# A quarter of the gate additions as matrix products, and background work spread over the steps, in a fused two-attention kernel

## The chip, the cores and the metric

The kernel runs on all 8 cores of one Trainium2 chip. Each core computes one of the 8 sequences with all weights; the cores don't talk to each other. The time is that of the slowest core, in device microseconds (us).

## The reference

One sequence has 2048 tokens of 1024 features. In short:

```
x = x + attn_a(layernorm(x))
x = x + ffn(layernorm(x))        # W rounded to 4 bits, bias, a rank-16 term
x = x + attn_b(layernorm(x))     # causal, 16 heads, rotary
x = x + ffn(layernorm(x))

attn_a, for each of 8 heads, q and k in two halves of 64, each of length 1:
  L1 = (q1 . k1) * c ;  L2 = (q2 . k2) * c          # 2048 x 2048
  G  = tanh(gain * (L1 - L2))                       # the gate
  A1 = softmax(L1 + G) ;  A2 = softmax(L2 - G)
  y  = (A1 - lam * A2) @ v ; y = y / rms(y) * w ; out = y @ Wo.T + bo
```

The change lies in attn_a: its two gate additions are L1 + G and L2 - G.

## The kernel before, in words

Each core goes through these stages: LayerNorm and the projections Q, K, V; the first attention (attn_a); the projections of the second attention; the second attention. The output projection of attn_a, the first ffn and the LayerNorms around them run as background work inside the first attention, for one pair of blocks of 128 tokens at a time.

PE is TensorE, DVE is VectorE, ACT is ScalarE, POOL is GpSimd. The program writes out the order of each engine's instructions by hand (`Seq`); `wait` makes the engine's queue wait for a semaphore, `done` returns the token to wait for. An engine works in this order strictly.

The first attention has 64 units: a head and 256 queries (`QA`). A unit has 8 steps (`NKS`) of 256 keys each, so there are 512 steps, and the 8 units (64 steps) of one group of 256 queries complete one pair of token blocks. Step s does the following, at different iterations of one loop:

- `step_D`: two products on PE give `pD`, the difference L1 - L2 times the gain, 128 keys x 512 columns (2 groups of keys x 256 queries). There is one `pD`. The factor is in `Qn`, made by `make_qn` on POOL.
- `step_tanh`: ACT writes `Gt`, the gate, from `pD`.
- `step_L`: four products of 64 rows on PE give L1 in bank `pL[2 * (s % 2)]` and L2 in the bank behind it, 128x512 each. They wait until the additions of step s - 2 have read these banks.
- `step_S`: DVE writes `Sx`, L1 + G and L2 - G, with two operations of 128x512.
- `step_exp`: ACT writes `E` from `Sx`, 128x1024 in one instruction.
- `step_Y`: eight products on PE add E's product with the values V to `pY`. At k = 1 of each unit no such products are issued, at k = 2 those of two steps.

At the end of a unit `y_out` copies `pY` to `Yt` on DVE, POOL normalizes it, `y_rms` sums squares on DVE, and `turn` transposes the result into Q by a DMA of SyncE's queue (SP). After eight units `turn` puts a generator `after_a` into the background.

A `Background` object runs these generators. A generator yields a cost after each piece: 1 for a product of 128x512, 0.3 for a small one, 0 to say that the rest of the work is for a later step. `step(budget)` takes pieces until the budget is used or a 0 comes. `out_proj` has 9 products, then an addition to x and LayerNorm statistics on DVE, for each half of a block; `ffn` has 8 small products, then 9 wide ones for each half. `layer_norm` computes the scale on POOL and applies it some steps later, on ACT, and for the last pair on DVE. At first the background holds `quantize` and `prepare`, which round the ffn's weights to 4 bits and scale Wo on DVE.

The order of the loop's work before (from `for s in range(-3, NS + NKS)`) is: tanh(s+2), exp(s), Y(s-1), one background step of budget 3, D(s+3), L(s+2), S(s+1). The background of the last pair runs in the next stage with a budget of 9, and the second attention has a background of its own with 3.

Of the kernel before, what the change touches and what calls it, by code (L numbers as in the profile page):

```python
# [33 lines left out]
E_RING = 4  # L34
# [185 lines left out]
class Background:  # L220
# [3 lines left out]
    def __init__(self):  # L224
        self.gens = deque()
        self.calls = []
        self.clock = 0

    def add(self, gen):
        self.gens.append(gen)  # L230
# [1 line left out]
    def later(self, steps, fn):  # L232
        self.calls.append((self.clock + steps, fn))

    def step(self, budget):
        self.clock += 1
        due = [c for c in self.calls if c[0] <= self.clock]
        self.calls = [c for c in self.calls if c[0] > self.clock]
        for _, fn in due:
            fn()  # L240
        while self.gens and budget > 0:
            cost = next(self.gens[0], None)
            if cost is None:
                self.gens.popleft()
                return
            if cost <= 0:
                return
            budget -= cost

    def drain(self):  # L250
        while self.gens or self.calls:
            self.step(1e9)


def build_program():
# [23 lines left out]
    dram_in("fb", (16, D))  # L279
    dram_in("cosb", (128, T))  # L280
    dram_in("sinbs", (128, T))
    for w in ("tri", "perm", "blk"):
        dram_in(w, (128, 128))
    d_out = nc.dram_tensor("out", [T, D], F32, kind="ExternalOutput").ap()
    d_x2 = nc.dram_tensor("x2", [T, D], F32, kind="Internal").ap()
# [389 lines left out]
    zz = sb("zz", (128, 2, 128), F32, s2a)  # L675
    yt = [sb(f"yt{i}", (128, 2, 128), BF16, s2a) for i in range(3)]
    cu = [sb(f"cu{i}", (128, 12), F32, s2a) for i in range(2)]
    p2 = contextlib.ExitStack()
    pL = [ps(f"pL{i}", p2) for i in range(4)]
    pD = ps("pD", p2)  # L680
# [1 line left out]
    pB = ps("pB", p2)  # L682

    ac.add(lambda e: e.preload_act_table_set("exp_and_others"))
    pe.wait(c2_tok)
    for ap, val in ((lora[0][0:96, :], 1.0), (lora[0][96:128, :], 0.0), (lora[1][0:96, :], 1.0),
                    (lora[1][96:128, :], 0.0), (sel[0:96, :], 0.0), (sel[96:128, :], 1.0),
                    (fbb[:, :], 0.0)):
# [66 lines left out]
    def out_proj(b, y_toks, w_tok, bias):  # L755

        tok = slice(128 * b, 128 * (b + 1))
        pe.wait(w_tok, *y_toks)
        for hf in range(2):
            cols = slice(512 * hf, 512 * (hf + 1))  # L760
            bank = state["banks"].take(pe)
            for c in range(NCH):
                mm(pe, bank[0], Q[:, c, tok], Wo[:, c, cols], c == 0, c == NCH - 1 and not bias)
                yield 1
            if bias:
                pe.wait(state["row97"])
                mm(pe, bank[0], sel[:, :], fbb[:, cols], False, True)
            p_tok = pe.done()
            yield 0
            ve.wait(p_tok, x_tok[b])  # L770
            tt(ve, x[:, b % 4, cols], bank[0], x[:, b % 4, cols], OP.add)
            bank[1] = ve.done()
            ve.wait(bank[1])
            ln_stats(b, hf)
            yield 0

    def layer_norm(b, q, i, then):


        g_tok = ln_aggr(b)  # L780

        def scale():
            po.wait(g_tok)
            ts(po, st[:, b, 14:15], st[:, b, 13:14], LN_EPS, OP.add)
            po.wait(po.done())
            tt(po, st[:, b, 15:16], st[:, b, 14:15], mhalf, OP.pow)
            tt(po, st[:, b, 16:17], st[:, b, 12:13], mone, OP.mult)
            po.wait(po.done())
            tt(po, st[:, b, 17:18], st[:, b, 16:17], st[:, b, 15:16], OP.mult)
            s_tok = po.done()  # L790
            bg.later(2, lambda: apply(s_tok))

        def apply(s_tok):
            q.wait(s_tok, xm_free[i])
            if q is ac:
                act(ac, xm[i], x[:, b % 4, :], AF.Identity, scale=st[:, b, 15:16],
                    bias=st[:, b, 17:18])
            else:
                ts(ve, xm[i], x[:, b % 4, :], st[:, b, 12:13], OP.subtract,
                   st[:, b, 15:16], OP.mult)  # L800
            then(q.done())

        bg.later(1, scale)
# [7 lines left out]
    def ffn(b, slot):  # L811

        nonlocal n_lora
        xt = xnT[:, :, 128 * slot:128 * (slot + 1)]
        while b not in xT_tok:
            yield 0
        pe.wait(xT_tok[b], state["wq"], state["row97"])
        k = n_lora % 2
        n_lora += 1
        bank = state["banks"].take(pe)  # L820
        for c in range(NCH):
            mm(pe, bank[0][0:16, 0:128], fab[:, c, :], xt[:, c, :], c == 0, c == NCH - 1)
            yield 0.3
        p_tok = pe.done()
        yield 0
        ve.wait(p_tok, lora_free[k])
        copy(ve, lora[k][0:16, :], bank[0][0:16, 0:128])
        bank[1] = l_tok = ve.done()
        yield 0
        for hf in range(2):  # L830
            cols = slice(512 * hf, 512 * (hf + 1))
            bank = state["banks"].take(pe)
            for c in range(NCH):
                mm(pe, bank[0], xt[:, c, :], wq[:, c, cols], c == 0, False)
                yield 1
            pe.wait(l_tok)
            mm(pe, bank[0], lora[k][:, :], fbb[:, cols], False, True)
            p_tok = pe.done()
            yield 0
            ve.wait(p_tok)  # L840
            stt(ve, x[:, b % 4, cols], bank[0], qscale[:, 0:1], x[:, b % 4, cols],
                OP.mult, OP.add)
            bank[1] = ve.done()
            ve.wait(bank[1])
            if state["ln3"]:
                ln_stats(b, hf)
            yield 0
        lora_free[k] = xT_free[slot] = p_tok
        state["x"] = bank[1]

    x2_tok = [None] * NTB
    xn3_tok = [None] * NTB
# [8 lines left out]
    def after_a(n, y_toks):  # L861

        last = n == NTB // 2 - 1
        q = ve if last else ac
        two = (2 * n, 2 * n + 1)
        if not last:
            load_x(di["xN"], 2 * n + 2)
            load_x(di["xN"], 2 * n + 3)
        for i, b in enumerate(two):
            yield from out_proj(b, y_toks, state["Wo"], True)  # L870
            layer_norm(b, q, i, lambda a_tok, b=b, i=i: turn_ln(b, i, a_tok, b % 4))
        if last:
            state["last_o"](pe.done())
        for i, b in enumerate(two):
            yield from ffn(b, b % 4)
            sy.wait(state["x"])
            x2_tok[b] = r_st.next(sy).start(sy, rows_of(d_x2, b), x[:, b % 4, :])
            layer_norm(b, q, 2 + i, lambda a_tok, b=b, i=i: keep(b, 2 + i, a_tok))
        while xn3_tok[two[1]] is None:
            yield 0  # L880
# [2 lines left out]
    bg = Background()  # L883
    units = [(t, qs, h) for t in range(NQT) for qs in range(2) for h in range(HA)]
    NS = len(units) * NKS
    L_tok, D_tok, G_tok, S_tok, E_tok = {}, {}, {}, {}, {}
    Y_tok, y_evac, yn_tok, qn_tok, yt_tok, zz_tok = {}, {}, {}, {}, {}, {}

    def q_range(u):
# [3 lines left out]
    def make_qn(u):  # L893
# [4 lines left out]
        tt(po, Qn[u % 2][:, :], Q[:, h, qsl], col_bc(gs[:, h:h + 1], QA), OP.mult)  # L898
        qn_tok[u] = po.done()

    def step_L(s):
        if not 0 <= s < NS:
            return
        h, qsl = q_range(s // NKS)
        pe.wait(S_tok.get(s - 2))
        for jj in range(2):
            j = 2 * (s % NKS) + jj
            js = slice(128 * j, 128 * (j + 1))
            cs = slice(QA * jj, QA * (jj + 1))
            mm(pe, pL[2 * (s % 2)][:, cs], K[0:64, h, js], Q[0:64, h, qsl], True, True, (0, 0))  # L910
            mm(pe, pL[2 * (s % 2) + 1][:, cs], K[64:128, h, js], Q[64:128, h, qsl], True, True,
               (64, 0))
        L_tok[s] = pe.done()

    def step_D(s):
        if not 0 <= s < NS:
# [10 lines left out]
    def step_tanh(s):  # L927
        if not 0 <= s < NS:
            return
        ac.wait(D_tok[s], S_tok.get(s - G_RING))  # L930
        act(ac, Gt[s % G_RING][:, :], pD[:, :], AF.Tanh)
        G_tok[s] = ac.done()

    def step_S(s):
# [2 lines left out]
        ve.wait(L_tok[s], G_tok[s], E_tok.get(s - S_RING))  # L937
        sx, gt = Sx[s % S_RING], Gt[s % G_RING]
        tt(ve, sx[:, 0, :], pL[2 * (s % 2)][:, :], gt[:, :], OP.add)
        tt(ve, sx[:, 1, :], pL[2 * (s % 2) + 1][:, :], gt[:, :], OP.subtract)  # L940
        S_tok[s] = ve.done()

    def step_exp(s):
        if not 0 <= s < NS:
            return
        ac.wait(S_tok[s], Y_tok.get(s - E_RING))
        act(ac, E[s % E_RING][:, :, :, :], Sx[s % S_RING][:, :, :], AF.Exp)
        E_tok[s] = ac.done()

    def step_Y(s):  # L950
# [76 lines left out]
    for s in range(-3, NS + NKS):  # L1027
# [5 lines left out]
        elif k == 2:  # L1033
            step_Y(s - 2)
            step_Y(s - 1)
        if s >= 0:
            bg.step(3)
        step_D(s + 3)
        step_L(s + 2)
        if u >= 0 and k == 1:  # L1040
            y_out(u, 1)
        step_S(s + 1)
        if u >= 0:
            if k == 0:
                y_out(u, 0)
# [6 lines left out]


    while len(bg.gens) > 1:
        bg.step(9)
    state["banks"].add(pD[:, :], G_tok[NS - 1])
    po.wait(Y_tok[NS - 1], S_tok[NS - 1], E_tok[NS - 1], yt_tok[len(units) - 1],
            yn_tok[len(units) - 1])
# [104 lines left out]
    for pair in range(2):  # L1163
        two = (2 * pair, 2 * pair + 1)
        for hf in range(2):
            for t in two:
                for h in range(4 * hf, 4 * hf + 4):
                    group_k(t, h)
                    if pair == 0:
                        bg.step(9)  # L1170
        if pair == 0:
            bg.drain()
            load_xs(2, xT_free[2], xT_free[3])
# [145 lines left out]
    for s in range(-2, NB + 5):  # L1319
# [6 lines left out]
                k = norm_b(t, c, i, s - 2)  # L1326
                turn_b(t, c, i, k)
        if s >= 0:
            bg.step(3)
        stepb_S(s + 2)  # L1330
    for k in range(4):
        state["banks"].add(pS[k // 2][:, k % 2, :], E_tok[NB - 1])
# [10 lines left out]
def _host_prep(inputs):  # L1343
# [59 lines left out]
```

How the kernel before makes its waits and increments, by code:

```python
    def wait(self, *tokens):  # L57
        for tok in tokens:
            if tok is None:
                continue
            sem, val = tok
            if self.seen.get(sem.name, 0) >= val:
                continue
            self.seen[sem.name] = val
            self.ops.append([lambda e, s=sem, v=val: e.wait_ge(s, v), None, 0])
# [11 lines left out]
    def emit(self, engine):  # L77
        for fn, sem, k in self.ops:
            inst = fn(engine)
            if sem is not None:
                inst.then_inc(sem, k)
```

## Time and profile before

| | us |
|---|---|
| median of 3 runs (lowest, highest) | 1842.59 (1841.95, 1843.29) |
| the profiled execution's own time | 1842.74 |
| its span, first to last instruction of the slowest core (core 5) | 1841.2 |
| busy PE / DVE / ACT / POOL in the span | 1483.1 / 1169.8 / 1272.7 / 511.9 |
| the first attention in it | 297.8 to about 1179 |

The profile is taken from one execution. Busy time is the union of an engine's instructions; the start and the end of neighbours may overlap, so what an instruction costs in a full stream is the time from its start to the start of the next. Where a row has "x4", four instructions in a row are merged. A figure in square brackets is the idle time of the engine before the instruction, with what ended it. Most additions, matmuls and activations go through helpers, so rows are told apart by their tiles, as `Sx<-pL,Gt`.

### The profile page before, as it was taken

The numbers are of one execution on the slowest core, as the hardware profiler recorded it, in microseconds if no ns is written. First come the engines' busy times: TensorE is split into PE (matmuls) and PEld (weight loads), VectorE is DVE, ScalarE is ACT, GpSimd is POOL, SyncE is SP. The second block draws the span as 40 slices with busy tenths as digits, with TensorE's granted clock in tenths as the row PEclk, the third lists the DMA queues.
The fourth block names the chain that finished last, engine by engine and source line by source line (L and its number), as shares of the span: only waits on it lengthen the run. The fifth ranks groups of instructions, "written<-read, shape, count | busy, mean of one in ns | idle before, by whom it ended". The sixth has DMA issues, their size and how long they took to land.

```text
span 1841.2 us, 39256 instructions; the slowest of 8 cores (1827.3 to 1841.2 us)
## 1 busy us (share of the span) xinstructions
PE 1483.1 (81%) x13024; PEld 757.6 (41%) x13024; DVE 1169.8 (64%) x2158; ACT 1272.7 (69%) x1699; POOL 511.9 (28%) x1055
## 2 busy tenths in 40 slices
PE   0467996778888888888888888569998799888977
PEld 0123443444444444444444444324443344343443
DVE  2235466998899989998998899534444353424214
ACT  1255574888999989989898998612333578787890
POOL 1000001444444544444444444423444000000000
PEclk9989998989999999999999999779999599999998
DMA  9711403211101011111101101177000513221302
GB/s 181 109 46 35 114 26 69 99 30 34 46 30 34 24 42 40 34 42 35 34 25 40 42 29 46 33 122 152 3 1 13 104 38 105 52 83 28 104 10 72
DMA packets 138392, 101.52 MB, mean 55 GB/s; under 512 B 107843, under 2 KB 122307, under 8 KB 138198
## 3 DMA queue, kind: packets, MB, share of 16 engines
q1 hardware_dynamic: 122166, 84.20, 17.2%
q0 software_dynamic: 16032, 14.81, 5.5%
q8 instruction: 112, 1.84, 0.4%
q14 instruction: 82, 0.67, 0.1%
HBM read 67.65 MB, written 20.97 MB: 48 GB/s over the span
## 4 chain that ended last, share of the span: by engine, by line
PE 32%; ACT 17%; DVE 13%; issue 12%; POOL 4%; DMA 3%; SPq 0%; DVEq 0%; POOLq 0%; ACTq 0%
ACT E L175 10%; DVE Sx L184 8%; PE pL L164 8%; PE pBb L164 6%; PE pS L166 4%; PE pYb L171 4%; ACT Gt L175 4%; ACT EB L175 3%; PE pY L171 3%; PE pB L164 3%; PE pL L166 2%; PE pD L164 2%; DMA V<-xn 1%; DVE x L184 1%; DMA Q<-yt 1%
## 5 line engine op out<-in xcount | busy, mean ns | idle before, releaser
L184 DVE TENSOR_TENSOR Sx<-pL,Gt 128x512 f32<-128x512 f32 x1024 | 649.0, 683 | 77.8 <-PE pL L166 41.9
L175 ACT ACTIVATE E<-Sx 128x1024 bf16<-128x1024 f32 x512 | 541.7, 1058 | 51.0 <-DVE Sx L184 48.5
L171 PE MATMUL pY<-V,E 128*128 128x129 bf16 x4096 | 311.3, 222 | 89.7 <-ACT E L175 78.7
L175 ACT ACTIVATE EB<-pS,cst 128x1024 bf16<-128x1024 f32 (+1 forms) x320 | 296.0, 992 | 78.1 <-PE pS L166 75.7
L175 ACT ACTIVATE Gt<-pD 128x512 bf16<-128x512 f32 x512 | 304.3, 594 | 41.5 <-PE pD L164 39.8
L171 PEld LDWEIGHTS pY<-V,E 128*128 128x128 bf16 x4096 | 240.6, 98 | 198.5 <-issue 198.4
L164 PE MATMUL pD<-Qn,K 128*128 128x256 bf16 x1024 | 198.1, 275 | 45.9 <-ACT Gt L175 38.9
L166 PE MATMUL pL<-Q,K 64*128 64x256 bf16 x2048 | 203.5, 277 | 9.5 <-DVE Sx L184 9.4
L171 PE MATMUL pYb<-V,EB 128*128 128x65 bf16 x2176 | 133.1, 200 | 10.0 <-DVE ytb L184 5.1
L166 PE MATMUL pS<-Q,K 64*128 64x512 bf16 (+3 forms) x640 | 121.2, 373 | 23.7 <-ACT EB L175 18.9
L175 ACT ACTIVATE qb<-pL 128x512 bf16<-128x512 f32 x64 | 38.1, 597 | 140.8 <-PE pL L164 137.1
L164 PE MATMUL pqk<-xn,w_q 128*128 128x512 bf16 x256 | 66.2, 407 | 79.0 <-DMA xn<-wq 79.0
L164 PEld LDWEIGHTS pD<-Qn,K 128*128 128x128 bf16 x1024 | 77.6, 97 | 114.1 <-issue 75.8
L189 POOL TENSOR_SCALAR st<-st 128x1 f32<-128x1 f32 x48 | 10.8, 225 | 407.8 <-DVE st L454 390.1
L171 PEld LDWEIGHTS pYb<-V,EB 128*128 128x128 bf16 x2176 | 90.4, 101 | 80.4 <-issue 74.0
L184 DVE TENSOR_TENSOR EB<-EB,c_tri 128x256 bf16<-128x256 bf16 x128 | 35.5, 290 | 132.9 <-ACT EB L175 122.9
L184 POOL TENSOR_TENSOR cu<-Yt,cst 128x2 f32<-128x2 f32 x64 | 44.0, 688 | 271.7 <-DVE Yt L199 271.7
L166 PEld LDWEIGHTS pL<-Q,K 64*128 64x128 bf16 x2048 | 59.3, 94 | 120.6 <-issue 120.5
L175 ACT ACTIVATE sqb<-pqk 128x512 bf16<-128x512 f32 x64 | 37.9, 592 | 82.0 <-PE pqk L164 81.7
L448 DVE BATCH_NORM_STATS2 st<-x 128x6 f32<-128x512 f32 x128 | 87.1, 691 | 11.0 <-DMA x<-xN 0.6
L184 DVE TENSOR_TENSOR ro<-pL,x 128x512 f32<-128x512 f32 x64 | 43.7, 682 | 76.1 <-ACT qb L175 55.4
L164 PE MATMUL pB<-Wo,Q 128*128 128x512 bf16 x240 | 68.3, 390 | 20.7 <-DMA Q<-yt 20.7
(155 smaller groups left out, 1951.4 us busy)
## 6 DMA issues: line engine op xcount, KB each, us to landing
x<-xN SPq DMA_DIRECT2D x32, 512.0 KB, 4.3
x<-x SPq DMA_DIRECT2D x32, 512.0 KB, 3.2
out<-x SPq DMA_DIRECT2D x16, 512.0 KB, 2.6
x<-fker SPq DMA_DIRECT2D x3, 2048.0 KB
x<-WoT SPq DMA_DIRECT2D x2, 2048.0 KB
xn<-xn SPq DMA_DIRECT2D x16, 256.0 KB, 2.1
w_q<-WqT POOLq DMA_DIRECT2D x2, 1024.0 KB, 21.5
w_k<-WkT POOLq DMA_DIRECT2D x2, 1024.0 KB, 44.3
```

Of the source, the lines that this page charges most:

```text
L164: q.add(lambda e: e.matmul(out, lhsT, rhs, start=start, stop=stop))
L166: q.add(lambda e: e.matmul(out, lhsT, rhs, start=start, stop=stop, tile_position=pos))
L171: q.add(lambda e: e.matmul(out, lhsT, rhs, start=first, stop=last, skip_group_check=True))
L175: q.add(lambda e: e.activation(out, in_, func, **kw))
L184: q.add(lambda e: e.tensor_tensor(out, a, b, op))
L189: q.add(lambda e: e.tensor_scalar(out, a, s1, None, op0))
L448: ve.add(lambda e: e.bn_stats(st[:, b, 6 * half:6 * half + 6], x[:, b % 4, 512 * half:512 * (half + 1)]))
```

## The change

Every odd step (`on_pe`) leaves L2 - G to PE: L2's products leave the accumulation open, and a fifth product adds -G to the bank, with a negative identity matrix `nident` as weights and `Gt` as the moving operand (`step_A`). ACT then takes the exponential of an odd step in two halves, the second half (L2 - G) straight from the bank, and first, then L1 + G from `Sx`. L of step s + 2 waits for this first half (`P_tok`), because the bank is free only then. A gate buffer is also held until the product has read it.

The loop's order becomes: tanh(s+2), exp(s), Y(s-1), D(s+3), L(s+2), A(s+1), S(s+1), one background step. The background gets a rate of 1.6 a step instead of a budget of 3, and may save up to 2.6 of it; costs beyond the credit are carried over. Statistics come one step after the addition to x; a LayerNorm is applied four steps after its scale instead of two, on DVE for all pairs. `nident` comes by a DMA of POOL's queue at the start of the stage and is negated on DVE. Elsewhere `bg.step(9)` and `bg.step(3)` become `bg.step(9, 9)` and `bg.step(3, 3)`.

```diff
-    def step(self, budget):
+    def step(self, rate, cap):
...
-        while self.gens and budget > 0:
+        self.credit = min(self.credit + rate, cap)
+        while self.gens and self.credit > 0:
             cost = next(self.gens[0], None)
...
-            budget -= cost
+            self.credit -= cost
...
     ac.add(lambda e: e.preload_act_table_set("exp_and_others"))
-    pe.wait(c2_tok)
+    i_tok = sl_c[0].start(po, nident[:, :], di["ident"])
+    ve.wait(i_tok)
+    ts(ve, nident[:, :], nident[:, :], -1.0, OP.mult)
+    pe.wait(c2_tok, ve.done())
...
             tt(ve, x[:, b % 4, cols], bank[0], x[:, b % 4, cols], OP.add)
             bank[1] = ve.done()
+            yield 0
             ve.wait(bank[1])
             ln_stats(b, hf)
-            yield 0
...
-            bg.later(2, lambda: apply(s_tok))
+            bg.later(4, lambda: apply(s_tok))
...
-            bank[1] = ve.done()
-            ve.wait(bank[1])
+            bank[1] = x_tok = ve.done()
+            yield 0
             if state["ln3"]:
+                ve.wait(x_tok)
                 ln_stats(b, hf)
-            yield 0
...
         last = n == NTB // 2 - 1
-        q = ve if last else ac
+        q = ve
...
+    def on_pe(s):
+
+        return s % 2 == 1
+
     def step_L(s):
...
-        pe.wait(S_tok.get(s - 2))
+        pe.wait(S_tok.get(s - 2), P_tok.get(s - 2))
...
-            mm(pe, pL[2 * (s % 2) + 1][:, cs], K[64:128, h, js], Q[64:128, h, qsl], True, True,
-               (64, 0))
+            if on_pe(s):
+                pe.add(lambda e, s=s, cs=cs, js=js, h=h, qsl=qsl, jj=jj: e.matmul(
+                    pL[2 * (s % 2) + 1][:, cs], K[64:128, h, js], Q[64:128, h, qsl],
+                    start=jj == 0, stop=False, tile_position=(64, 0), skip_group_check=True))
+            else:
+                mm(pe, pL[2 * (s % 2) + 1][:, cs], K[64:128, h, js], Q[64:128, h, qsl], True, True,
+                   (64, 0))
         L_tok[s] = pe.done()
+
+    def step_A(s):
+
+        if not 0 <= s < NS or not on_pe(s):
+            return
+        pe.wait(G_tok[s])
+        mm_in(pe, pL[2 * (s % 2) + 1][:, :], nident[:, :], Gt[s % G_RING][:, :], False, True)
+        A_tok[s] = pe.done()
...
-        ac.wait(D_tok[s], S_tok.get(s - G_RING))
+        ac.wait(D_tok[s], S_tok.get(s - G_RING), A_tok.get(s - G_RING))
...
-        tt(ve, sx[:, 1, :], pL[2 * (s % 2) + 1][:, :], gt[:, :], OP.subtract)
+        if not on_pe(s):
+            tt(ve, sx[:, 1, :], pL[2 * (s % 2) + 1][:, :], gt[:, :], OP.subtract)
...
-        ac.wait(S_tok[s], Y_tok.get(s - E_RING))
-        act(ac, E[s % E_RING][:, :, :, :], Sx[s % S_RING][:, :, :], AF.Exp)
+        e = E[s % E_RING]
+        ac.wait(Y_tok.get(s - E_RING))
+        if on_pe(s):
+            ac.wait(A_tok[s])
+            act(ac, e[:, 1, :, :], pL[2 * (s % 2) + 1][:, :], AF.Exp)
+            P_tok[s] = ac.done()
+            ac.wait(S_tok[s])
+            act(ac, e[:, 0, :, :], Sx[s % S_RING][:, 0, :], AF.Exp)
+        else:
+            ac.wait(S_tok[s])
+            act(ac, e[:, :, :, :], Sx[s % S_RING][:, :, :], AF.Exp)
...
-        if s >= 0:
-            bg.step(3)
         step_D(s + 3)
         step_L(s + 2)
+        step_A(s + 1)
         if u >= 0 and k == 1:
             y_out(u, 1)
         step_S(s + 1)
+        if s >= 0:
+            bg.step(1.6, 2.6)
```

## Rows read from the trace of the kernel before

**Rows 1.** Stretches: length, busy time of each engine, granted clock, DMA share.

```profile
core 5: us, PE busy (x) PEld busy (x) DVE busy (x) ACT busy (x) POOL busy (x), PEclk, DMA share, GB/s
297.75:410.15 112.40, 82.36 (x872) 47.29 (x872) 104.66 (x174) 93.66 (x126) 42.56 (x83) 0.90 0.22 62
519.00:628.00 109.00, 92.45 (x990) 52.51 (x987) 98.96 (x176) 99.40 (x133) 48.69 (x113) 1.00 0.12 35
...
```

**Rows 2.** Groups of instructions, 519 to 955 us.

```profile
L184 DVE TENSOR_TENSOR Sx<-pL,Gt 128x512 f32<-128x512 f32 x514 | 325.9, 682 | 35.0 <-PE pL L166 24.2 <-ACT E L175 5.3 <-ACT Gt L175 0.6
L175 ACT ACTIVATE E<-Sx 128x1024 bf16<-128x1024 f32 x257 | 272.0, 1058 | 19.4 <-DVE Sx L184 18.0 <-DVE Yt L199 0.9
```

**Rows 3.** Timeline of ACT, steps without background work: start, length.

```profile
637.10 0.64 ACT L175 ACTIVATE Gt<-pD 128x512 bf16<-128x512 f32 x1
637.72 1.06 ACT L175 ACTIVATE E<-Sx 128x1024 bf16<-128x1024 f32 x1
...
640.10 0.59 ACT L175 ACTIVATE Gt<-pD 128x512 bf16<-128x512 f32 x1
640.58 1.06 ACT L175 ACTIVATE E<-Sx 128x1024 bf16<-128x1024 f32 x1
641.53 0.60 ACT L175 ACTIVATE Gt<-pD 128x512 bf16<-128x512 f32 x1
```

**Rows 4.** Waits, 519 to 1178 us: us in total, times, longest.

```profile
ACT E L175 <- DVE Sx L184: 28.0, 41, 1.1
...
ACT Gt L175 <- PE pD L164: 24.4, 69, 1.7
```

**Rows 5.** Timeline of PE: a quiet step, then steps with background products.

```profile
640.35 0.61 PE L171 MATMUL pY<-V,E 128*128 128x129 bf16 x8 [0.24 <-ACT E L175]
640.84 0.38 PE L164 MATMUL pD<-Qn,K 128*128 128x256 bf16 x2
...
646.45 0.81 PE L164 MATMUL pB<-Wo,Q 128*128 128x512 bf16 x3 [1.19 <-DMA Q<-yt]
647.10 0.38 PE L164 MATMUL pD<-Qn,K 128*128 128x256 bf16 x2
647.41 0.39 PE L166 MATMUL pL<-Q,K 64*128 64x256 bf16 x4
647.74 0.63 PE L171 MATMUL pY<-V,E 128*128 128x129 bf16 x8
...
653.18 0.81 PE L164 MATMUL pB<-Wo,Q 128*128 128x512 bf16 x3
...
660.49 0.81 PE L164 MATMUL pB<-Wo,Q 128*128 128x512 bf16 x3
```

**Rows 6.** Timeline of DVE, around a background addition.

```profile
658.21 0.68 DVE L184 TENSOR_TENSOR x<-pB,x 128x512 f32<-128x512 f32 x1
658.99 0.69 DVE L448 BATCH_NORM_STATS2 st<-x 128x6 f32<-128x512 f32 x1
...
661.15 2.48 DVE L184 TENSOR_TENSOR Sx<-pL,Gt 128x512 f32<-128x512 f32 x4
```

**Rows 7.** Instructions on tile xn after 300 us: ns min/median/max, first and last start.

```profile
L175 ACT ACTIVATE xn<-x,st x28: 1225/1237/1242, 448.8 to 1153.8; 128x1024 bf16<-128x1024 f32 x28
...
L191 DVE TENSOR_SCALAR xn<-x,st x4: 804/808/812, 1239.3 to 1273.2; 128x1024 bf16<-128x1024 f32 x4
```

**Rows 8.** Groups of ACT before 290 us: an exponential from SBUF.

```profile
L175 ACT ACTIVATE rn<-rn 128x512 f32<-128x512 f32 x32 | 20.2, 630 | 2.9
```

**Rows 9.** Timeline of DVE in the stage's first steps.

```profile
303.65 1.28 DVE L184 TENSOR_TENSOR Sx<-pL,Gt 128x512 f32<-128x512 f32 x2
305.04 0.69 DVE L189 TENSOR_SCALAR wq<-x 128x1024 bf16<-128x1024 f32 x1
305.65 1.28 DVE L184 TENSOR_TENSOR Sx<-pL,Gt 128x512 f32<-128x512 f32 x2
```

**Rows 10.** Timeline at the start of the first attention.

```profile
295.40 0.88 POOL L120 DMA_DIRECT2D wkb<-WkB  x1 [0.58 <-POOLq L65]
...
297.06 0.59 PE L164 MATMUL pD<-Qn,K 128*128 128x256 bf16 x2 [6.16 <-POOL Qn L184]
...
297.75 0.60 ACT L175 ACTIVATE Gt<-pD 128x512 bf16<-128x512 f32 x1 [4.57 <-PE pD L164]
```

More of the change, by code:

```diff
@@ L227, in __init__ @@
         self.clock = 0
+        self.credit = 0.0
     def add(self, gen):
@@ L247, in step @@
                 return
-            budget -= cost
+            self.credit -= cost
     def drain(self):
         while self.gens or self.calls:
-            self.step(1e9)
+            self.step(1e9, 1e9)
+        self.credit = 0.0
 def build_program():
@@ L281, in build_program @@
     dram_in("sinbs", (128, T))
-    for w in ("tri", "perm", "blk"):
+    for w in ("tri", "perm", "blk", "ident"):
         dram_in(w, (128, 128))
@@ L677, in build_program @@
     cu = [sb(f"cu{i}", (128, 12), F32, s2a) for i in range(2)]
+    nident = sb("nident", (128, 128), BF16, s2a)
     p2 = contextlib.ExitStack()
@@ L842, in ffn @@
                 OP.mult, OP.add)
-            bank[1] = ve.done()
-            ve.wait(bank[1])
+            bank[1] = x_tok = ve.done()
+            yield 0
             if state["ln3"]:
+                ve.wait(x_tok)
                 ln_stats(b, hf)
-            yield 0
         lora_free[k] = xT_free[slot] = p_tok
-        state["x"] = bank[1]
+        state["x"] = x_tok
     x2_tok = [None] * NTB
@@ L885, in build_program @@
     NS = len(units) * NKS
-    L_tok, D_tok, G_tok, S_tok, E_tok = {}, {}, {}, {}, {}
+    L_tok, D_tok, G_tok, S_tok, E_tok, A_tok, P_tok = {}, {}, {}, {}, {}, {}, {}
     Y_tok, y_evac, yn_tok, qn_tok, yt_tok, zz_tok = {}, {}, {}, {}, {}, {}
@@ L1054, in build_program @@
     while len(bg.gens) > 1:
-        bg.step(9)
+        bg.step(9, 9)
     state["banks"].add(pD[:, :], G_tok[NS - 1])
@@ L1169, in build_program @@
                     if pair == 0:
-                        bg.step(9)
+                        bg.step(9, 9)
         if pair == 0:
@@ L1328, in build_program @@
         if s >= 0:
-            bg.step(3)
+            bg.step(3, 3)
         stepb_S(s + 2)
@@ L1383, in _host_prep @@
     com["perm"] = pm
+    com["ident"] = np.ascontiguousarray(np.eye(128, dtype=f))
     com["blk"] = (idx[:, None] // 64 == idx[None, :] // 64).astype(f)
```

## The prediction

> **What bounds the kernel now.** I read the busy times of equal stretches first. The first attention runs from 297.8 to about 1179 us, almost half the span, and repeats every 109 us in its middle [rows 1]: the 436 us from 519 to 955 hold 257 exponentials and 514 additions [rows 2], so 109 us are 64 steps (one pair of token blocks), 1.70 us a step. No engine is full: of 109 us DVE is busy 99, ACT 99, PE 92.5 [rows 1].
>
> The timeline of ACT shows why. In a quiet step (no background work) it runs without a gap: tanh at 640.10, exponential at 640.58, next tanh at 641.53. A tanh takes 0.475 us of ACT, an exponential 0.95, and once in eight steps 0.14 is added (637.10 to 637.72), where two steps' value products stand together [rows 3]. Quiet pace for 64 steps: 64 x 1.425 + 8 x 0.14 = 92.3 us. The other 16.7 of the 109 come with background work. There ACT waits for DVE's Sx and for pD [rows 4]. The reader is to see in PE's timeline three background products (0.65 us) between the transposed value products and D, so that the next tanh gets its logits late [rows 5]; and in DVE's timeline an x and an st operation, 0.78 and about 0.6 us, between two pairs of additions [rows 6].
>
> Sums for 64 steps, from start to next start. DVE: 128 additions x 0.60 (four in 2.48 us) = 77; copies and a reduction about 1.0 for each of 8 units; background 2 blocks x 6.1 = 12: 97. ACT: 64 x 1.425 + 4 LayerNorm applications of 1.24 less 0.11 of overlap [rows 7] = 95.7. PE: Y 0.48, D 0.31, L 0.32 make 1.11 a step [rows 5], 71; 72 wide background products x 0.216, and small ones 0.9: 87.5.
>
> **The change, part by part.**
> *Additions.* 256 of 1024 go, 154 us of DVE at 0.60. Per 64 steps DVE falls by 19, and takes four LayerNorm applications from ACT at 0.81 each [rows 7]: 81. It stops being a bound. ACT loses 4 x 1.13 = 4.5.
>
> *The product in their place* is 128x512, 0.216 to the next start by the background's [rows 5]: 32 x 0.216 = 6.9 us per 64 steps. It stands behind the 64-row products, where the switch of shape is paid already. PE: 94.4.
>
> *The exponential cut in two.* The half from PSUM resembles tanh, 0.59; the half from SBUF resembles rn<-rn, 0.63 [rows 3, 8]. Together 1.22 against 1.058 for the whole [rows 2], less one more overlap of 0.12 as between tanh and exponential: +0.045 in each odd step, 1.4 us per 64. Bounds: nothing, and 0.165 without overlap.
> The Trainium skill (ScalarE: Activation LUTs, What ACT_TABLE_LOAD costs) gives an activation 186 ns of fixed cost and 93 of overlap, so one more costs 93 ns: by it 3.0 us per 64 steps where the rows give 1.4. No row here shows a half exponential.
>
> *Order.* D, L and the new product now precede the background products, S precedes DVE's background work. Take a quiet odd step s with tanh(s+2) at 0: Y(s-1) starts at 0.25, D at 0.74 [rows 3, 5], L followed at 1.05. Now L(s+2) also waits for the PSUM half of exponential s: it starts at 0.48, ends at 1.07, and PE sees it 0.14 later, as it sees E for Y: 1.21. L is issued by 1.53, and Y(s) can't start before 1.73 (second half 0.955 to 1.585, plus 0.14), so the new wait is covered. In the even step Y, D, L and the product start at 1.73, 2.21, 2.52 and 2.84; the product lands 0.38 later and ACT sees it after 0.10 more (pD ends 297.65, tanh starts 297.75 [rows 10]): 3.32. The exponential that wants it starts at 0.48 + 2.90 = 3.38. That is covered by 0.06 only. Queued behind a late product are both halves and the next tanh on ACT; through the PSUM half, the L of two steps later on PE.
>
> *Background spread.* From the generators' costs, rate 1.6 with cap 2.6 gives 3, 2, 1, 2, 1, 0 products: nine in six steps where it was 3, 3, 3, 0 in four. Stepping the generators on paper, a pair's work fills 58 of 64 steps (40 before) and ends before the next pair's begins, so nothing piles up for the end. Eight groups fill 48 steps. In six steps PE has 6 x 1.11 + (3 + 9) x 0.216 = 9.25 us, ACT 6 x 1.425 + 3 x 0.045 = 8.7: a group becomes PE's. Today a four-step group takes 6.73 and 7.31 (646.45, 653.18, 660.49) [rows 5], where DVE's sum, the largest, is 4 x 1.2 + 1.4 + 0.5 = 6.7: up to 9% over. With that the new group takes 10.05, packed perfectly 9.25. I take the middle, 9.65: ACT starves only when D is more than 0.2 late (it may start at 0.95 instead of 0.74), and background now follows D.
>
> Per 64 steps: 8 x 9.65 + 16 x 1.46 = 100.6; 1.4 for the first product's wait on transposed values (1.2 us of idle PE at 646.45 today, then with D and L already done), small products, borders of units and DVE's applications: 102.0. Check against today: 92.3 + 8 x (7.0 - 5.7) + 4.5 + 1.9 = 109.1, as measured. Gain 7.0 x 7 pairs = 49 us.
> The Trainium skill (TensorE: Matmul & The Clock Gate, Back-to-back issue gap) gives 131 ns for a sustained 512-column product. The rows' 216 disagrees. By 131 the 32 products would add 4.2 rather than 6.9 us.
>
> *First 64 steps.* They take 112.4 us [rows 1]. Quantization and the scaling of Wo put one DVE operation of about 0.7 us into some 24 of them: pairs of additions at 303.65 and 305.65 [rows 9]. With half of every second pair gone, two such steps need 3 x 0.60 + 2 x 0.7 = 3.2 instead of 3.9 us: 0.3 x 24 = 7, halves included. Wo is loaded eight steps ahead of use; shorter steps shrink that margin, a stall of 2 us is the bound.
>
> *Setup.* One more DMA issue on POOL stands ahead of the memsets and Qn, which release the first D: 0.88 us as wkb's [rows 10]. Its landing, DVE's negation and PE's wait for it run beside the memsets. I take 1 us, bound 3.
> *Elsewhere.* The rates 9 and 3 give the same steps as before, since a product costs 1; statistics one step later and LayerNorm two steps later lie behind other blocks' products, and without that cover would cost two steps per pair. SP and POOL issue nothing else new: 0.
>
> Sum against the profiled execution's 1842.7 (median 1842.6): 49 + 7 - 1 = 55 less: 1788 us.
>
> **Rivals.**
> A. *PE takes half of it back.* Groups at 10.05, halves without overlap in the 16 steps that ACT paces. For: PE will be the fullest engine, 94.4 of 102. 8 x 10.05 + 16 x 1.46 + 1.4 = 105.2: gain 3.8 x 7 = 27. Halves without overlap cost 8 odd steps x 0.12 more per 64, 8 over the stage; the first steps give 3, setup takes 2: 27 - 8 + 3 - 2 = 20, so 1823. Chance 0.2.
> B. *Near perfect packing.* Groups at 9.3: 99.2 per 64, gain 69 + 8 - 1: 1767. For: where PE is late it leaves no gap between D, L and Y (647.10, 647.41, 647.74) [rows 5]. Against: DMA waits and unit borders. 0.1.
> C. *The new chain decides, and it is slower.* Product, PSUM half, its release, L into the same bank form a loop that needs 2.84 of the 2.90 us of two steps. If each hand-over takes a little longer than those I know, the excess comes in every odd step. With the product's landing fully exposed (0.38 + 0.10 less 0.06 of cover, 0.42): 256 x 0.42 = 108 on 1788, 1896; with half of it, 1842. So it turns to slower from 55/256 = 0.215 us per odd step; at 0.3 it gives 1865. Against: every hand-over in it has its row, 0.10 and 0.14. 0.09.
> D. *No change.* ACT's waits for pD become waits for the product in equal number: groups of 10.5, first steps as now: 1842. Nothing in the rows asks for so much. 0.03.
> E. Mine: 0.58.
>
> **Numbers.** My own case reaches from 1774 (groups 9.4) to 1806 (9.9 and small first steps). The range 1765 to 1824 takes in A and B, leaving out C, D and the edges. What a measurement of this kernel tells from no change is 0.2%, 3.7 us. Faster 0.58 + 0.2 + 0.1 = 0.88, same 0.03, slower 0.09.
>
> **What would show it.** Right: 768 additions; 64 steps in about 102 us with DVE busy near 81; quiet steps 1.43 and 1.47 apart; inside groups PE without idle. Wrong in C's way: ACT waits for PE pL, or PE pL for ACT E, in most steps, quiet ones too. Wrong otherwise: Sx still releasing ACT, half exponentials well over 0.63, more than 1.11 us of PE per step from the longer list of waits, or a granted clock under 1.00 in the repeating part, where it is 1.00 today [rows 1].

## The result, and the profile after

The changed kernel takes 1794.16 us, median of 4 runs (1790.24 to 1794.87); the kernel before 1842.94 beside it. The ratio is 0.973, 95% interval 0.9713 to 0.9747: 49 us faster, where 55 were forecast. Runs and cores in which one half of the chip had a lower granted clock are left out of every comparison; for the experiments e8, e11 and e12 this leaves too few runs for an interval, so their profiles carry the reading.

I cut the span at the first tanh, the last exponential of the first attention, the 17th `qb` copy of the next stage, and the first and last exponential of the second attention. First the stretches after the first attention in the kernel before, then all stretches after the change (length, busy time of PE, its weight loads, DVE, ACT, POOL, granted clock, DMA share, GB/s):

```profile
1179.04:1299.16 120.12, 85.07 (x378) 37.17 (x379) 36.35 (x61) 19.16 (x33) 35.69 (x49) 0.84 0.64 115
...
1423.59:1794.12 370.53, 319.31 (x3310) 151.59 (x3309) 127.50 (x359) 296.00 (x320) 15.97 (x51) 0.91 0.26 66
1794.12:1841.20 47.08, 36.42 (x180) 15.89 (x177) 23.14 (x41) 0.00 (x0) 4.55 (x16) 0.86 0.24 70
```

```profile
297.45:1123.49 826.04, 750.38 (x7901) 440.20 (x8030) 673.91 (x1166) 785.74 (x1280) 385.44 (x867) 0.99 0.15 41
1123.49:1257.21 133.72, 85.85 (x371) 37.53 (x379) 36.09 (x61) 19.14 (x32) 35.47 (x49) 0.81 0.60 105
...
1381.74:1747.72 365.98, 314.07 (x3268) 151.72 (x3310) 126.58 (x359) 296.08 (x320) 15.99 (x51) 0.91 0.28 67
1747.72:1793.20 45.48, 34.99 (x170) 15.51 (x174) 22.50 (x42) 0.00 (x0) 5.83 (x16) 0.92 0.26 73
```

The first attention fell from 881.3 to 826.0: 55.3 us. The stage behind it grew from 120.1 to 133.7; the second attention and the last stretch became shorter by 4.6 and 1.6. So the first attention alone gained more than the whole kernel did, some 14 us were given back in a stage to which I had given nothing, and 6 came from the two stretches at the end.

The stretches of 64 steps that answer to [rows 1]:

```profile
297.40:401.30 103.90, 84.50 (x887) 49.15 (x903) 87.64 (x143) 94.36 (x158) 42.72 (x84) 0.93 0.24 67
504.00:606.60 102.60, 95.04 (x1000) 55.75 (x1016) 83.71 (x147) 98.48 (x161) 48.99 (x113) 1.00 0.13 38
```

102.6 us where 109.0 stood; DVE from 99 to 84 busy, PE from 92.5 to 95.0, ACT hardly changed. Groups of instructions between 504 and 914 us, answering to [rows 2] (L923 is the line of L2's products in odd steps):

```profile
L184 DVE TENSOR_TENSOR Sx<-pL,Gt 128x512 f32<-128x512 f32 x383 | 251.1, 685 | 67.3 <-PE pL L923 29.0 <-PE pL L166 28.1 <-ACT E L175 8.5
...
L175 ACT ACTIVATE E<-Sx 128x1024 bf16<-128x1024 f32 x128 | 135.6, 1060 | 3.9 <-DVE Sx L184 3.9
...
L175 ACT ACTIVATE E<-Sx 128x512 bf16<-128x512 f32 x127 | 79.9, 629 | 0.0
L175 ACT ACTIVATE E<-pL 128x512 bf16<-128x512 f32 x127 | 76.4, 601 | 2.8
```

The halves last 629 and 601 ns, where 630 and 594 were taken from other instructions. Above all, ACT hardly waits for DVE any more: 3.9 us in 410, 18.0 in 436 before. Now it is DVE that idles, 67 us. ACT's timeline in a quiet step, to be held against [rows 3]:

```profile
607.79 0.62 ACT L175 ACTIVATE Gt<-pD 128x512 bf16<-128x512 f32 x1
608.26 0.63 ACT L175 ACTIVATE E<-pL 128x512 bf16<-128x512 f32 x1
608.74 0.67 ACT L175 ACTIVATE E<-Sx 128x512 bf16<-128x512 f32 x1
609.26 0.64 ACT L175 ACTIVATE Gt<-pD 128x512 bf16<-128x512 f32 x1
```

An odd step takes 1.47 us, tanh to tanh, without a gap. PE's timeline at the start of a group of nine background products, against [rows 5]:

```profile
519.33 0.81 PE L164 MATMUL pB<-Wo,Q 128*128 128x512 bf16 x3 [0.51 <-DMA Q<-yt]
519.98 0.62 PE L171 MATMUL pY<-V,E 128*128 128x129 bf16 x8
520.43 0.38 PE L164 MATMUL pD<-Qn,K 128*128 128x256 bf16 x2
520.74 0.39 PE L166 MATMUL pL<-Q,K 64*128 64x256 bf16 x4
521.07 0.39 PE L171 MATMUL pL<-Gt,nident 128*128 128x512 bf16 x1
521.29 0.59 PE L164 MATMUL pB<-Wo,Q 128*128 128x512 bf16 x2
521.73 0.38 PE L164 MATMUL pD<-Qn,K 128*128 128x256 bf16 x2
522.29 0.27 PE L166 MATMUL pL<-Q,K 64*128 64x256 bf16 x1 [0.19 <-ACT E L175]
...
529.03 0.82 PE L164 MATMUL pB<-Wo,Q 128*128 128x512 bf16 x3
```

The reader is to see three things. The product takes 0.22 us to the next start (521.07 to 521.29). L of the odd step waits for the PSUM half, with PE idle for 0.19 us: this is the new wait, and it isn't always covered. Between 504 and 915 us, with 128 odd steps, it is seen 48 times:

```profile
PE pL L166 <- ACT E L175: 8.4, 48, 0.3
```

And the group lasts 9.70 us, from 519.33 to 529.03, for a forecast of 9.65.

### The profile page after: what moved, and what is told of

It reads as the page before. It is cut to its first block, busy times and chain, and to the rows that moved or that the text cites. A ratio compares the mean times of both kernels' runs of the same rounds, so it can differ in the third digit from the quotient of the medians.

```text
span 1793.2 us, 40041 instructions; the slowest of 8 cores (1779.0 to 1793.2 us)
## 1 busy us (share of the span) xinstructions
PE 1494.7 (83%) x13069; PEld 781.9 (44%) x13280; DVE 1043.6 (58%) x1931; ACT 1267.1 (71%) x1927; POOL 516.8 (29%) x1056
## 4 chain that ended last, share of the span: by engine, by line
PE 39%; ACT 23%; issue 12%; DVE 4%; DMA 4%; POOL 1%; SPq 1%; ACTq 0%; DVEq 0%; POOLq 0%
ACT E L175 12%; PE pL L164 9%; ACT Gt L175 7%; PE pY L171 6%; PE pBb L164 5%; PE pB L164 4%; ACT EB L175 4%; PE pS L166 4%; PE pYb L171 4%; PE pL L166 3%; PE pD L164 3%; DMA V<-xn 2%; DVE Sx L184 1%; PE pS L164 1%; DMA xn<-xn 1%
## 5 line engine op out<-in xcount | busy, mean ns | idle before, releaser
L184 DVE TENSOR_TENSOR Sx<-pL,Gt 128x512 f32<-128x512 f32 x768 | 503.3, 684 | 138.1 <-PE pL L923 55.3
L175 ACT ACTIVATE E<-Sx 128x1024 bf16<-128x1024 f32 (+1 forms) x512 | 433.0, 846 | 13.0 <-DVE Sx L184 12.7
L175 ACT ACTIVATE EB<-pS,cst 128x1024 bf16<-128x1024 f32 (+1 forms) x320 | 296.1, 988 | 73.5 <-PE pS L166 69.0
L171 PEld LDWEIGHTS pY<-V,E 128*128 128x128 bf16 x4096 | 259.3, 98 | 91.5 <-issue 39.2
L166 PE MATMUL pL<-Q,K 64*128 64x256 bf16 x1536 | 199.0, 274 | 24.8 <-ACT E L175 16.6
L175 ACT ACTIVATE E<-pL 128x512 bf16<-128x512 f32 x256 | 154.1, 602 | 6.1 <-PE pL L166 0.9
L923 PE MATMUL pL<-Q,K 64*128 64x256 bf16 x512 | 100.1, 276 | 0.0
L164 PE MATMUL pB<-Wo,Q 128*128 128x512 bf16 x240 | 73.0, 390 | 20.0 <-DMA Q<-yt 13.7
```

Of the source, the lines that this page charges most:

```text
L164: q.add(lambda e: e.matmul(out, lhsT, rhs, start=start, stop=stop))
L166: q.add(lambda e: e.matmul(out, lhsT, rhs, start=start, stop=stop, tile_position=pos))
L171: q.add(lambda e: e.matmul(out, lhsT, rhs, start=first, stop=last, skip_group_check=True))
L175: q.add(lambda e: e.activation(out, in_, func, **kw))
L184: q.add(lambda e: e.tensor_tensor(out, a, b, op))
L923: pe.add(lambda e, s=s, cs=cs, js=js, h=h, qsl=qsl, jj=jj: e.matmul(pL[2 * (s % 2) + 1][:, cs], K[64:128, h, js], Q[64:128, h, qsl], start ...
```

## Where the 14 us were given back

PE, POOL's DMA issues and SP's transposition around the last pair's first small products; the kernel before, then after. The DMA rows are merged (x2), so their second figure reaches from the first issue to the end of the second and is not the time of a transfer:

```profile
1240.19 15.90 SPq L127 DMA_TRANSPOSE xn<-xn  x2
...
1243.43 1.01 PE L164 MATMUL pB<-xn,fab 128*16 128x128 bf16 x8 [2.94 <-DMA xn<-xn]
...
1244.00 1.85 POOL L120 DMA_DIRECT2D Wo<-WqB  x2
```

```profile
1188.06 2.00 POOL L120 DMA_DIRECT2D Wo<-WqB  x2
...
1189.71 30.06 SPq L127 DMA_TRANSPOSE xn<-xn  x2
...
1204.09 1.01 PE L164 MATMUL pB<-xn,fab 128*16 128x128 bf16 x8 [16.24 <-DMA xn<-xn]
```

Before, the transposition of the normalized block was issued at 1240.19, ahead of the two 1 MB loads of WqB at 1244.00, and PE waited 2.9 us. A LayerNorm applied two steps later puts it 1.65 us behind these loads, and PE waits 16.2 us. The stretches inside this wait show the granted clock and how full the DMA engines are (a share of 1.30 says that the times of the packets add up to more than the 16 engines' time, so packets were under way side by side):

```profile
1195.00:1200.00 5.00, 0.00 (x0) 0.00 (x0) 0.00 (x0) 0.00 (x0) 0.00 (x0) 0.50 1.30 159
1200.00:1205.00 5.00, 0.91 (x8) 0.76 (x8) 0.00 (x0) 0.00 (x0) 0.00 (x0) 0.50 1.12 181
```

## The experiments

In this table a stage's length is the median over the 8 cores of the profiled execution (for e2 and e11 over cores 4 to 7), from the same marks as above; "64 steps" is the third stretch of 64 steps in the first attention. The experiments ran on several chips, and the kernel before takes 1845, 1849 and 1845 us on those of e1 to e4, of e5 to e8 and of e10 to e13. So times are compared by their ratio to the kernel before on the same chip; a ratio times 1842.9 gives the time to hold against the 1794 of the changed kernel.

| kernel | time, ratio to before | first 64 steps | 64 steps | first attention | next stage to the 17th copy | second attention |
|---|---|---|---|---|---|---|
| before | 1842.9 | 112.5 | 108.8 | 879.5 | 118.4 | 369.1 |
| after | 1794.2, 0.973 | 103.8 | 102.6 | 824.5 | 130.6 | 364.6 |
| e1 | 0.9703 | 103.8 | 102.5 | 824.0 | 120.5 | 372.4 |
| e2 | 0.9679 | 104.2 | 102.6 | 825.0 | 123.7 | 364.6 |
| e3 | 0.9798 | 111.0 | 104.2 | 839.2 | 130.3 | 364.1 |
| e4 | 0.9859 | 104.0 | 105.8 | 847.5 | 132.1 | 363.6 |
| e5 | 0.9821 | 105.1 | 105.0 | 842.5 | 132.4 | 363.3 |
| e6 | 0.9901 | 103.8 | 107.5 | 857.0 | 130.5 | 363.9 |
| e7 | 0.9908 | 105.0 | 107.8 | 861.1 | 121.0 | 366.4 |
| e8 | 1850.5 in the profile | 106.4 | 110.0 | 873.9 | 131.1 | 364.6 |
| e10 | 1.0007 | 112.2 | 109.6 | 881.3 | 127.5 | 363.4 |
| e11 | 1853.7 in one run | 107.8 | 110.7 | 885.2 | 129.5 | 363.9 |
| e12 | 1780.7 in the profile | 103.8 | 102.6 | 824.6 | 120.5 | 365.1 |
| e13 | 0.9581 | 107.3 | 100.0 | 809.9 | 120.3 | 365.7 |

### e1: LayerNorm two steps after its scale again, everywhere

```diff
-            bg.later(4, lambda: apply(s_tok))
+            bg.later(2, lambda: apply(s_tok))
```

> A LayerNorm is applied two steps after its scale again instead of four; all else as changed. The first attention gained its forecast 55 us but the next stage grew by about 11, where PE waits 16.2 us for the transposed xn of the last pair's first block, issued 1.6 us after the two 1 MB loads of WqB. Theory (the transposition stands behind these loads in the DMA engines): issued before them again it lands in 3 to 4 us, the stage shrinks by about 12, time 1794 - 12 = 1782. Rival (the later statistics and the split background steps made that stage longer, not the LayerNorm's place): 1792 to 1796.

Measured: median 1789.1, ratio 0.9703 (0.9681 to 0.9725), where 1782 was expected. That is 5 us under the changed kernel, and the two intervals overlap, so it isn't clear of noise. PE's small products wait 2.9 us again, and the next stage is 10 us shorter, as the theory says. But the second attention takes 372.4 instead of 364.6. The theory was right about its own stage, and there was a second effect that neither side expected, of nearly the same size. The second attention is even 3.3 us longer than in the kernel before, and 6.0 longer than in e7, which has the two steps with the statistics at their old place. So with two steps the later statistics seem to cost something there; no run isolates it.

```profile
1187.09 1.01 PE L164 MATMUL pB<-xn,fab 128*16 128x128 bf16 x8 [2.94 <-DMA xn<-xn]
```

### e2: the loads of WqB behind the transpositions

```diff
-        if last:
-            state["last_o"](pe.done())
+        o_tok = pe.done()
         for i, b in enumerate(two):
             yield from ffn(b, b % 4)
+            if last and i == 0:
+                state["last_o"](o_tok)
```

> The changed kernel with the late LayerNorm kept, but the loads of WqB are issued only after the first block's ffn products, so behind both transpositions. Theory (order of the DMAs): the small products wait 2 to 4 us instead of 16, time about 1783. Rival (the two steps of delay are themselves the cost, whatever the DMA engines do): two steps are some 4 us, so the time stays at 1790 or above.

Measured: ratio 0.9679 (0.9656 to 0.9702), three runs at 1783.9, 1784.8 and 1788.1; PE's wait for the transposed block 5.1 us instead of 16.2, the next stage 7 us shorter, the second attention unchanged. With the LayerNorm as late as in the changed kernel, the order of the two kinds of DMA alone removes most of the loss. PE still waits 2.2 us longer than with two steps (5.1 against 2.9); whether the lateness or the later loads leave these 2 to 3 us isn't told apart.

### e3: no products in place of additions

```diff
     def on_pe(s):
-        return s % 2 == 1
+        return False
```

> No step leaves its addition to PE, exponentials are whole; order, spreading and the rest as changed. Theory (DVE was the bound together with the bursts, and PE is it now): DVE's sum returns to 100 us per 64 steps, with the old 5 to 8% on top inside groups 105 to 106 us per 64 steps instead of 102.6, first 64 steps back near 110, time 1794 + 20 + 6, about 1820. Rival (order and spreading bring all the gain, the additions are hidden): 1788 to 1797, by the saved products and half exponentials even below the changed kernel.

Measured: ratio 0.9798 (0.9774 to 0.9821), median 1806.6: 12 us slower than the changed kernel, half of what was expected, and well clear of the rival. It is still 37 us faster than the kernel before: three quarters of the gain of 49 need no product at all. The first 64 steps are back at 111.0, but the later ones stand at 104.2 only. The stretch shows DVE at 99.9 of 104.2 us busy: with background behind D, L and S, DVE runs nearly full.

```profile
511.10:615.29 104.19, 92.64 (x984) 51.84 (x984) 99.94 (x179) 94.81 (x130) 48.80 (x113) 1.00 0.12 37
```

### e4: background in bursts

```diff
-            bg.step(1.6, 2.6)
+            bg.step(3, 3)
```

> Background steps of three products at once (rate and cap 3) in the new place; all else as changed. Theory (spreading is worth something because a three-product step makes PE late by more than the 0.2 us of slack): four-step groups at 7.1 plus two quiet steps of 1.47 make 10.0 instead of about 9.7 per nine products, 8 x 0.3 per 64 steps, so 1794 + 17, about 1808. Rival (the place behind D and L is all that counts): 1792 to 1797.

Measured: ratio 0.9859 (0.9835 to 0.9883), median 1818.8, 24 us slower than the changed kernel by the ratios. The first attention is 23 us longer; spreading is worth that much, more than the 14 expected. The rival, that the place is all, is out.

### e5: background ahead of D and L

```diff
+        if s >= 0:
+            bg.step(1.6, 2.6)
         step_D(s + 3)
         step_L(s + 2)
         step_A(s + 1)
         if u >= 0 and k == 1:
             y_out(u, 1)
         step_S(s + 1)
-        if s >= 0:
-            bg.step(1.6, 2.6)
```

> The background step stands ahead of D and L again, still at rate 1.6 and cap 2.6; all else as changed. Theory (D may start 0.2 us late before ACT starves, and background ahead of it uses this up): two or three products ahead of D (0.43, 0.65 us) starve ACT by 0.2 to 0.4, three times in a six-step group, 8 groups: 3 to 5 us per 64 steps, time about 1794 + 28 = 1822. Rival (spreading alone brings the gain, the place is of no account because PE sums the same): 1792 to 1798.

Measured: ratio 0.9821 (0.9807 to 0.9836), median 1816.4 on a chip where the kernel before takes 1849. By the ratios it is 17 us slower than the changed kernel, where 28 were expected and none to 4 by the rival, which is out. The place alone is worth 18 us of the first attention.

### e6: LayerNorm applied on ACT

```diff
-        q = ve
+        q = ve if last else ac
```

> LayerNorm is applied on ACT again for all pairs but the last; all else as changed. Theory (ACT has some 3% of slack inside groups, since PE sets their pace, and none outside): of 4 x 1.13 us per pair about half shows, time 1794 + 7 x 2.3 = 1810. Rival (PE's pace hides them whole): 1792 to 1797.

Measured: ratio 0.9901 (0.988 to 0.9922), median 1830.3, 32 us slower by the ratios where 16 were expected. Both were wrong. 64 steps take 4.9 us more in the stretch of the table and 4.6 in the mean of the seven later ones, so the whole of the four applications shows (4 x 1.13 = 4.5): ACT has no room for them. An application is one piece of 1.24 us, though, and what it delays next is a tanh: between 504 and 915 us PE's D waits for the tanh 15.2 us, against 3.6 in the changed kernel. So the runs don't say whether the same time in small pieces would cost as much. It is the largest single part of the change.

```profile
508.40:616.17 107.77, 97.08 (x1004) 56.85 (x1016) 81.06 (x143) 102.58 (x166) 48.41 (x113) 0.98 0.12 36
```

### e7: the products alone

The kernel before with `step_A`, the halved exponentials and `nident`; order, budget, LayerNorm and statistics as before.

```diff
-        if s >= 0:
-            bg.step(1.6, 2.6)
...
+        if s >= 0:
+            bg.step(3, 3)
         step_D(s + 3)
...
-        q = ve
+        q = ve if last else ac
...
-            bg.later(4, lambda: apply(s_tok))
+            bg.later(2, lambda: apply(s_tok))
```

> Only the products in place of a quarter of the additions, with the halved exponentials and the extra DMA; order, budget 3, LayerNorm and statistics as before the change. Theory (D's lateness behind three products rules this order, DVE is second): only the steps in which DVE was last get shorter; the first 64 steps, all DVE's, fall by 8, the others by about 1.5 each, less 1.4 for halves: 8 to 15 us off 1843, about 1831. Rival (the freed 154 us of DVE are the main cause of the gain): 25 to 45 us off, 1798 to 1818.

Measured: ratio 0.9908 (0.9892 to 0.9925), 17 us off where 8 to 15 were expected and 25 to 45 by the rival; the first attention 18 us shorter, of which 7.5 in the first 64 steps and 1.0 to 2.5 in each later 64 (1.5 in the mean). The 154 us of additions taken from DVE, for themselves, bring about a tenth of that.

### e8: the product twice

```diff
-    ts(ve, nident[:, :], nident[:, :], -1.0, OP.mult)
+    ts(ve, nident[:, :], nident[:, :], -0.5, OP.mult)
...
+        mm_in(pe, pL[2 * (s % 2) + 1][:, :], nident[:, :], Gt[s % G_RING][:, :], False, False)
         mm_in(pe, pL[2 * (s % 2) + 1][:, :], nident[:, :], Gt[s % G_RING][:, :], False, True)
```

> Each product of the gate is issued twice with half the weights, so each odd step costs PE 0.216 us more and its bank is ready 0.216 later; the result is the same sum. Theory (PE sets the pace of the 48 group steps of 64, and the chain product, PSUM half, L has next to no cover elsewhere): 24 x 0.216 + 8 x 0.15 = 6.4 us per 64 steps, 51 over the stage, time about 1845. Rival (ACT's sum is the bound and PE has room): under 15 us more, 1796 to 1809.

Measured: 1850.5 in the profiled execution and 1848.7 in another, with 1848.9 for the kernel before on that chip. The first attention takes 49 us more than after the change, as the theory said, and the rival is out. 32 more products of 0.216 us, 6.9 in all, make 64 steps 7.4 us longer (6.7 in the mean of the seven later stretches). The edit does two things at once, though: it takes PE's time, and it makes the bank ready later. Between 504 and 915 us ACT now waits for the product in 85 of some 120 odd steps, and PE for the release in 76, where the changed kernel's ACT idles before that half 2.8 us in all and its PE waits 48 times for the release:

```profile
ACT E L175 <- PE pL L171: 19.2, 85, 0.3
PE pL L166 <- ACT E L175: 15.4, 76, 0.5
```

So whether PE has no room for the time of a product or the chain none for its lateness, e8 doesn't tell.

### e10: the kernel before with the late LayerNorm

```diff
-            bg.later(2, lambda: apply(s_tok))
+            bg.later(4, lambda: apply(s_tok))
```

> The kernel before with one thing changed: a LayerNorm is applied four steps after its scale instead of two, everywhere. Theory (the place behind the loads of WqB costs the stage after the first attention 12 us by itself; in the second attention the later place helps, since an application that waits for POOL's scale holds up DVE): first attention unchanged within 2, next stage 94 to 106 us, second attention 369 to 364; in all 1843 + 12 - 5 = 1850. Rival (the second attention's gain comes from the statistics' new place): 1854 to 1857.

Measured: ratio 1.0007 (0.9987 to 1.0027), so no change where 7 us more were expected. One line moves three stages and the sum is nothing: the next stage is 9 us longer where 12 were expected (PE waits 12.7 us for the transposed block), the second attention 5.7 shorter, the end 2.8 shorter, which I hadn't expected. The statistics' new place has no part in the second attention's gain. Its waits show how it comes, kernel before and then e10 (second attention; us, times, longest):

```profile
PE pBb L164 <- DVE x L184: 10.2, 12, 1.4
...
DVE xn L191 <- POOL st L184: 5.3, 3, 2.0
```

```profile
PE pBb L164 <- DVE x L184: 4.3, 10, 0.6
...
DVE xn L191 <- POOL st L184: 1.6, 1, 1.6
```

With two steps DVE reaches the application before POOL has the scale; behind it stands DVE's read of the one background bank, for which PE waits.

### e11: the half from PSUM second

```diff
-            ac.wait(A_tok[s])
-            act(ac, e[:, 1, :, :], pL[2 * (s % 2) + 1][:, :], AF.Exp)
-            P_tok[s] = ac.done()
             ac.wait(S_tok[s])
             act(ac, e[:, 0, :, :], Sx[s % S_RING][:, 0, :], AF.Exp)
+            ac.wait(A_tok[s])
+            act(ac, e[:, 1, :, :], pL[2 * (s % 2) + 1][:, :], AF.Exp)
+            P_tok[s] = ac.done()
```

> In odd steps ACT takes the half from Sx first, then the half from PSUM, so the bank is released 0.52 us later and the product has 0.52 us more time; all else as changed. Theory (L of two steps later waits for the release, and PE, fully loaded inside groups, can't take a gap): PE idles up to 0.5 us in every odd step before L; 24 x 0.35 + 8 x 0.1 us in 64 steps where it isn't already late, some 8 us per 64, 1794 + 60, about 1855. Rival (the product's lateness is the tight side, the release has slack): 1785 to 1797.

Measured on cores 4 to 7 of the profiled execution: the first attention takes 885 us, 60 more than the changed kernel, as the theory said; 64 steps take 110.7 instead of 102.6. The one run that can be compared takes 1853.7, for an expected 1855; the rival is out. PE's row (core 6) shows the place:

```profile
607.53 0.27 PE L166 MATMUL pL<-Q,K 64*128 64x256 bf16 x1 [0.55 <-ACT E L175]
```

### e12: two steps for the last pair, four elsewhere

```diff
-            bg.later(4, lambda: apply(s_tok))
+            bg.later(2 if state["ln3"] and b >= NTB - 2 else 4, lambda: apply(s_tok))
```

> The changed kernel with two steps instead of four for the last pair's LayerNorms only, four elsewhere. Theory: the next stage falls back from 106 to about 95 us, the second attention keeps its 365: 1794 - 12 = 1782. Rival (as with four steps replaced by two everywhere, the second attention loses again what the next stage gains): 1788 to 1792.

Measured: 1780.7 in the profiled execution, 1784.8 in another run, for an expected 1782. Next stage 120.5, second attention 365.1: both effects are had, and the rival is out.

```profile
1188.43 1.01 PE L164 MATMUL pB<-xn,fab 128*16 128x128 bf16 x8 [2.91 <-DMA xn<-xn]
```

### e13: half as many products

```diff
     def on_pe(s):
-        return s % 2 == 1
+        return s % 4 == 1
```

On top of e12's edit.

> As the kernel with two steps for the last pair only, but the product takes one addition in every fourth step instead of every second, so an eighth of them. Theory (PE and ACT are both charged for a product, 0.216 and 0.07 us, DVE's sum falls far below theirs, so the best share lies lower than a quarter): per 64 steps 3.5 us less of PE, DVE at 92 of 102; first 64 steps 4 us longer, later ones 0 to 1 shorter: 1782 + 0 to 4, the same as that kernel. Rival (DVE needs all of the relief): half of the 15 us that the products brought is lost, 1789.

Measured: ratio 0.9581 (0.9558 to 0.9604), median 1768.5, from 1765.0 to 1770.0. It beats both kernels, and e12 by some 13 us. The first 64 steps are 3.5 us longer than with twice the products, each later 64 are 2.6 shorter:

```profile
295.87:404.10 108.23, 87.73 (x888) 49.10 (x888) 95.80 (x158) 93.84 (x143) 41.70 (x84) 0.90 0.23 64
...
503.75:603.82 100.07, 94.86 (x1004) 53.88 (x1000) 91.98 (x163) 96.08 (x145) 48.89 (x113) 1.00 0.14 39
```

My theory had the direction for the repeating steps and mis-sized it: 0 to 1 us expected.

## Why the prediction held, point by point

*What bounded the kernel.* Right: bursts of products ahead of D and pairs of DVE operations between additions. e5 (18 us), e4 (23) and e6 (32) undo one part each; e3 undoes the additions and loses 15, all in the first attention. These add up to more than 55: the parts depend on each other, and how isn't shown.

*Repeating steps.* 7.0 us per 64 forecast, 6.2 measured in the stretch of the table (108.8 to 102.6) and 6.6 in the mean of the seven. The group of nine products at 9.65 was measured as 9.70, 9.71 and 9.44, with 9.91 where small products follow.

*First 64 steps.* 7 us forecast, 8.7 measured (my 3.9 should read 3.8, by 4 x 0.60 + 2 x 0.7; the 0.3 per step stands). Setup 1 forecast, 0.6 measured (first tanh at 295.5 and 296.1, medians of cores that lie up to 4 us apart). So the first attention came to 55 us for a forecast of 56 with 46 for 49 in its repeating part: two errors that partly cancel, which is luck.

*Halved exponentials.* 0.045 us per odd step forecast. In a quiet odd step the halves cost 0.48 and 0.52 and the whole 0.95 (608.26 to 609.26 against [rows 3]): 0.05. The Trainium skill's 93 ns (ScalarE: Activation LUTs, What ACT_TABLE_LOAD costs) would be nearly twice that. The rows show where the difference lies: two halves like the one from Sx would cost 2 x 0.52 - 0.95 = 0.09, an estimate that agrees with the skill's figure, and the half that reads PSUM is cheaper by 0.04.

*The product.* 0.216 us to the next start, 0.22 measured. The Trainium skill's 131 ns for a sustained 512-column product (TensorE: Matmul & The Clock Gate, Back-to-back issue gap) isn't borne out here.

*The step that failed* is the line "Elsewhere": "statistics one step later and LayerNorm two steps later lie behind other blocks' products". In the stage after the first attention they don't: the later application put the transposition behind 2 MB of weight loads. Undone for the last pair alone (e12) that gives 10 us back. The same line missed 4.6 and 1.6 us of gain in the second attention and after it; e10 shows both. My zero was the sum of +12 and -6, from the medians of the cores, and it is nearly all of the 6 us by which my total of 55 was too high.

*Where a right number hid a wrong reason.* I wrote that inside groups PE sets the pace and ACT has room, 8.7 of 9.25 us, and that PE would be without idle there. PE does idle there (522.29), and e6 contradicts the room: 4.5 us more on ACT cost 4.6. e8 adds 6.9 on PE and pays 6.7. So both engines are charged nearly in full, though PE is busy 95 of 102.6 us. What then sets the pace isn't shown.

A candidate is the loop through both: product, PSUM half, its release, L into the same bank, with tanh and D beside it. I had it as rival C, at 2.84 of 2.90 us, and used it only to ask whether quiet steps would hold. For it: its waits are seen 48 times (8.4 us in 411), e8 makes the product's end later and its waits the commonest of PE and ACT, and e11 makes the release 0.52 us later per two steps and pays 60 us of the 133 that 256 times 0.52 would be. Against it as the bound of the changed kernel: those 8.4 us are 2.1 per 64 steps, and of the chain of work that ended last, followed back through 504 to 606.6 us, the product makes up 0.6%; exponentials and tanh on ACT make up 40%, and Y, background, L and D on PE 33%. So rival C's mechanism is there, far below the 0.215 us per odd step from which it would have turned the result; e13, which halves the number of such loops, takes 15 us more from the first attention. How these 15 divide among the products left out (128 x 0.216 = 28 us of PE), the halved exponentials and the waits for the release, the runs don't tell apart.

*Rivals A, B and D* are out: groups lasted 9.4 to 9.9, mostly 9.7, not 10.05, 9.3 or 10.5, and the first attention gained 55 us where A needs 22 and B 77.

## What to carry to other kernels

Moving work from a full engine to one with room isn't priced by the two engines' sums; the chain that it forms with its neighbours counts too: a quarter of the additions brought 15 us of the first attention next to 154 us of DVE time removed, and an eighth of them 29 (e3, e12 and e13). Background work goes behind the instructions that another engine waits for, and spread over the steps; place and spreading were worth 18 and 23 us. A delay counted in steps is also an order among DMAs: list for each stage what is issued between the old and the new place, above all bulk loads, before calling it free.

## What the runs showed of the hardware

A transposition of 256 KB issued 1.65 us behind two loads of 1 MB, on another queue, landed 14 us after its issue instead of 3 to 4: it did not pass them. While PE waited 16.2 us for it, its granted clock fell to 0.50, the lower of the two levels (1.2 GHz), and stood there at the restart (1200 to 1205). An exponential of 128x512 costs ACT 0.48 us from start to start when it reads PSUM and 0.52 when it reads SBUF (608.26, 608.74, 609.26).
